# Graph network on one core: two of each tile's four adjacency scatters in the message pass, the others in edge order beside the first convolution

## The reference, cut to what matters

```python
x = _layernorm(x + _L0_gnn_ref(x, src, dst, ...))                 # softmax over the edges of a node
x = _layernorm(x + _L1_gnn_ref(x, edge_index, edge_attr_4, ...))  # a message of each edge, summed
x = _layernorm(x + _L2_gnn_ref(x, edge_index, ...))               # two convolutions, relu between
x = _layernorm(x + _L3_gnn_ref(x, edge_index, ...))               # two convolutions, elu between

def _sage_conv(h, src, dst, Wl, bl, Wr, num_nodes):
    agg = _mean_aggr(h, src, dst, num_nodes)   # mean of h[src] over the edges that end at a node
    return agg @ Wl.T + bl + h @ Wr.T
```

## Time and profile before

| | |
|---|---|
| median of 3 runs | 5566.3 us (5557.26 to 5571.82) |
| the profiled execution, its own time | 5569.94 us |
| its span, first to last instruction | 5568.1 us |
| mean granted TensorE clock | 0.818 |
| PE, DVE, ACT, POOL busy | 58%, 49%, 28%, 45% |

### The profile page before, as it was taken

How to read it: one execution, slowest core, us unless ns; L and a number is a source line. 1 busy time by engine, 2 the same in 40 slices (tenths; PEclk the granted TensorE clock), 3 DMA queues, 4 the chain that set the end, 5 groups by cost and what they waited for, 6 DMA issues and landing times.

```text
span 5568.1 us, 71606 instructions
## 1 busy us (share of the span) xinstructions
PE 3216.9 (58%) x18541; PEld 2357.2 (42%) x18541; DVE 2708.7 (49%) x6211; ACT 1578.4 (28%) x3821; POOL 2483.5 (45%) x2580
## 2 busy tenths in 40 slices
PE   0444444444464454454444445443118999999999
PEld 0333233333343333333333333332106887778877
DVE  3777777777644444444444444436313234433333
ACT  1666666666222222222222222222000001111000
POOL 6555555555555566656555655666760000000000
PEclk9999999999986666666666666655558999999999
DMA  6555555555223333333333333332014666666676
GB/s 202 168 178 181 166 180 180 170 178 168 64 73 87 87 97 89 87 87 90 86 91 84 95 88 89 85 88 54 2 44 172 248 249 247 245 249 251 254 276 231
DMA packets 411992, 801.65 MB, mean 144 GB/s; under 512 B 237480, under 2 KB 288396, under 8 KB 385692
## 3 DMA queue, kind: packets, MB, share of 16 engines
q1 hardware_dynamic: 263894, 591.99, 31.8%
q0 software_dynamic: 82320, 90.28, 7.8%
q10 hardware_dynamic: 65718, 118.62, 5.6%
HBM read 581.84 MB, written 218.74 MB: 144 GB/s over the span
## 4 chain that ended last, share of the span: by engine, by line
another core or an unknown queue 30%; PE 27%; issue 17%; ACT 12%; DVE 8%; ACTq 3%; POOL 1%; SPq 1%; DMA 0%; DVEq 0%; POOLq 0%
PE ps L991 22%; ACT ps L1040 2%; ACT dump L1044 2%; ACT out_ring L1056 2%; ACT relu_dump L1040 2%; DVE second L1474 2%; ACT second L1081 1%; PE ps L953 1%; ACT out_ring L1064 1%; ACTq L1066 1%; DVE area L1490 1%; ACT ps L1076 1%; ACTq L1060 1%; DVE second L1484 1%
## 5 line engine op out<-in xcount | busy, mean ns | idle before, releaser
L843 PE MATMUL ps<-ident,area 96*128 96x96 f32 x2352 | 441.3, 355 | 1154.6 <-ACT out_ring L1056 425.5
L693 POOL DMA_INDIRECT area<-src_table,idx_src x784 | 750.5, 957 | 525.1 <-DMA idx_src<-src_dram 270.3
L693 POOL DMA_INDIRECT area<-relu_table,idx_src x784 | 739.5, 943 | 537.3 <-issue 336.1
L843 PEld LDWEIGHTS ps<-ident,area 96*128 96x128 f32 x2352 | 352.1, 211 | 1281.3 <-issue 957.8
L1461 DVE TENSOR_TENSOR_SCAN area<-flags,area,ps 96x512 f32<-96x512 int8 x196 | 249.8, 1274 | 1213.5 <-ACT dump L1044 1007.4
L704 POOL DMA_INDIRECT adj<-copies_ring,cell_ring x587 | 578.1, 985 | 378.0 <-DVE cell_ring L1442 198.4
L991 PE MATMUL ps<-early,area 128*128 128x288 bf16 x5194 | 665.8, 287 | 1.6 <-DVE early L1606 1.6
L991 PE MATMUL ps<-second,area 128*128 128x288 bf16 x5194 | 651.2, 286 | 0.5 <-DVE second L1606 0.5
L991 PEld LDWEIGHTS ps<-early,area 128*128 128x128 f16 x5194 | 508.9, 98 | 129.8 <-issue 2.1
L991 PEld LDWEIGHTS ps<-second,area 128*128 128x128 f16 x5194 | 508.2, 98 | 128.1 <-DVE second L1606 1.1
L1426 DVE SCALAR_TENSOR_TENSOR second<-second,area,ps 128x512 bf16<-128x512 f32 x784 | 538.6, 743 | 0.0
(11 more groups left out here) (298 smaller groups left out, 4555.1 us busy)
## 6 DMA issues: line engine op xcount, KB each, us to landing
area<-adj SPq DMA_DIRECT2D x196, 1632.0 KB
adj<-early SPq DMA_DIRECT2D x102, 816.0 KB
soft_sums<-out_ring ACTq DMA_DIRECT2D x196, 384.0 KB
second<-key_dram SPq DMA_DIRECT2D x98, 512.0 KB
area<-dst_table SPq DMA_DIRECT2D x784, 48.0 KB
sums<-out_ring ACTq DMA_DIRECT2D x196, 192.0 KB
second<-caps_dram SPq DMA_DIRECT2D x98, 192.0 KB
attr<-attr_parts SPq DMA_DIRECT2D x196, 72.0 KB
```

The source lines that it names most:

```text
L693: pool.indirect_dma_start(out=src_rows[:, s, c, :], out_offset=None, in_=gather_table[p], in_offset=bass.IndirectOffsetOnAxis(ap=idx_src[s ...
L843: last = nc.tensor.transpose(ps[:, b, c * F:(c + 1) * F], r[:, (s * CH + c) * P:(s * CH + c + 1) * P], ident[0:F, 0:F])
```

## The change

`NOW` becomes 2, and in tile t the message pass scatters chunks 2t and 2t+1 of the sorted edges, whose copies were counted in a tile already done. So the 196 tiles scatter the first 392 chunks (`EARLY`), half of all. The other 390 are scattered by POOL after the gathers of the ends, in edge order, in batches of eight (`BATCH`), and after each batch has landed POOL raises `adj_ready`. DVE prepares them in one go after the pass (`cell_late`, `copies_late`, in the space of `out_ring`). A table `tile_ready` of 49 numbers, made from the degrees in the setup by three small DVE operations, tells how many batches each row of tiles needs.

The first convolution no longer waits for the joint rows. SP's `fill_first` loads 49 blocks of row j when the batches that it needs are there (a register loaded from `tile_ready`), PE's `sum_up_first` sums them, and DVE's `hold` adds the result, times `rdeg`, to `z_sb`. Then the two joint rows are summed, which needs all batches. Then comes a second step for all 49 tiles: SP loads the two columns of tying blocks of all rows in one DMA (`links`, pieces of 512 bytes), PE's `link` multiplies them with the parts of the joint rows (six matmuls a tile), DVE's `post` adds the result to `z_sb` into `layer_out`, and PE turns and projects it for the second convolution, with ACT and DVE as in the first projection. `over_jobs` takes its number of jobs as an argument, ACT evicts tile k before it keeps the z of tile k-1, and the search in the setup waits for its rows two groups at a time, which frees semaphores. The later convolutions are as before.

```diff
 REPEAT = 1024
-NOW = CH - 1
+NOW = 2
...
+    EARLY = ET * NOW
+    LATE = CN - EARLY
+    BATCHES = math.ceil((SCATTERS - EARLY) / BATCH)
+    assert LATE > 0 and SCATTERS > EARLY
...
+        def over_first_jobs(step, eng):
+            over_jobs(step, eng, jobs=NT, head=SLOTS + 1)
+
+        def uses_of_slot(lane, q):
+
+            return (len(range(lane, NT, SLOTS)) + (1 if lane < EXT else 0) + len(range(lane, JOBS, SLOTS)) * (q - 1)) if q else 0
...
 
 
-            sp.wait_ge(adj_made, 16 * (SCATTERS + EXT))
             sp.wait_ge(node[-1]["kept"], NG)
-            for q in range(CONVS):
+
+            def fill_first(j, lane, nth):
+                if not (isinstance(j, int) and j < SLOTS):
+                    sp.wait_ge(conv["summed_up"], j - (SLOTS - 1))
+                batches = nc.values_load(tile_ready[0:1, bass.ds(j, 1)], engines=[mybir.EngineType.SP], min_val=1,
+                                         max_val=BATCHES + 1)
+                sp.wait_ge(adj_ready, batches)
+                sp.dma_start(slots[:, lane, 0:NT, :].rearrange("p b n -> p (b n)"),
+                             adj[bass.ds(j, 1), :, 0:NT * P].rearrange("a p c -> (a p) c")).then_inc(slot_landed[lane], 16)
+
+            over_first_jobs(fill_first, sp)
+
+            sp.wait_ge(adj_ready, BATCHES + 1)
+            for i in range(EXT):
+                sp.wait_ge(conv["summed_up"], NT - SLOTS + 1 + (i - NT) % SLOTS)
+                sp.dma_start(slots[:, i, 0:NT, :].rearrange("p b n -> p (b n)"), adj[NT + i, :, 0:NT * P])\
+                  .then_inc(slot_landed[i], 16)
+            sp.wait_ge(conv["summed_up"], NT - 1)
+            sp.dma_start(links, adj[0:NT, :, NT * P:KB * P].rearrange("t p (e n) -> p t e n", e=EXT)).then_inc(links_landed, 16)
+
...
-                    pool.sem_inc(scatters_begun, 1)
+                    pool.sem_inc(dmas_begun, 1)
                     for c in range(NOW):
-                        if isinstance(u, int) and (u * RING + s) * CH + c >= SCATTERS:
-                            return
                         pool.indirect_dma_start(
                             out=adj_all, out_offset=bass.IndirectOffsetOnAxis(ap=cell_ring[:, s, c:c + 1], axis=0),
...
-                    pool.wait_ge(last_redirected, 2)
-                    for c in range(NOW, SCATTERS, CH):
-                        pool.indirect_dma_start(
-                            out=adj_all, out_offset=bass.IndirectOffsetOnAxis(ap=cell[:, c:c + 1], axis=0),
-                            in_=copies_last[:, c // CH:c // CH + 1], in_offset=None).then_inc(adj_made, 16)
+                    pool.wait_ge(late_redirected, 2)
+
+                    def batch_done(i):
+                        begun = sum(min(BATCH, SCATTERS - EARLY - k * BATCH) for k in range(i % 2, i + 1, 2))
+                        pool.wait_ge(late_made[i % 2], 16 * begun)
+                        pool.sem_inc(adj_ready, 1)
+
+                    pool.wait_ge(adj_made, 16 * (EARLY + EXT))
+                    pool.sem_inc(adj_ready, 1)
+                    for i in range(BATCHES):
+                        for c in range(i * BATCH, min((i + 1) * BATCH, SCATTERS - EARLY)):
+                            pool.indirect_dma_start(
+                                out=adj_all, out_offset=bass.IndirectOffsetOnAxis(ap=cell_late[:, c:c + 1], axis=0),
+                                in_=copies_late[:, c:c + 1], in_offset=None).then_inc(late_made[i % 2], 16)
+                        if i:
+                            batch_done(i - 1)
...
-            for q in range(CONVS):
+            y = parts_of_y[0]
+
+            def sum_up_first(j, lane, nth):
+                pe.wait_ge(slot_landed[lane], nth * 16 + 16)
+
+                wait(pe, conv["reduced"], j - 1)
+                if isinstance(j, int) and j == 0:
+                    pe.wait_ge(conv["split"], NT)
+                for s in range(NT):
+                    last = nc.tensor.matmul(bank(lane % 2, P, PARTS_F), slots[:, lane, s, :],
+                                            y[:, s, :, :].rearrange("p c f -> p (c f)"), start=s == 0, stop=s == NT - 1)
+                last.then_inc(conv["summed_up"], 1)
+
+            over_first_jobs(sum_up_first, pe)
+
+            for i in range(EXT):
+                pe.wait_ge(slot_landed[i], 16 * uses_of_slot(i, 1))
+                pe.wait_ge(conv["reduced"], NT + i - 1)
+                for s in range(NT):
+                    last = nc.tensor.matmul(bank((NT + i) % 2, P, PARTS_F), slots[:, i, s, :],
+                                            y[:, s, :, :].rearrange("p c f -> p (c f)"), start=s == 0, stop=s == NT - 1)
+                last.then_inc(conv["summed_up"], 1)
...
+            pe.wait_ge(conv["extended"], EXT)
+
+            def link(k):
+
+                wait(pe, conv["posted"], k - 1)
+                for e in range(EXT):
+                    for c in range(PARTS):
+                        last = nc.tensor.matmul(bank(6 + k % 2, P, F), links[:, k, e, :], y[:, NT + e, c, :],
+                                                start=e == 0 and c == 0, stop=e == EXT - 1 and c == PARTS - 1)
+                last.then_inc(linked, 1)
+
+            for k in range(NT + 2):
+                if k < NT:
+                    link(k)
+                if 1 <= k <= NT:
+                    pe.wait_ge(conv["posted"], k)
+                    turn_into(1, k - 1, (k - 1) % 2, layer_out[:, (k - 1) % 2, :])
+                if k >= 2:
+                    project_into(1, k - 2, k % 2)
+
+            for q in range(1, CONVS):
...
 
-            for k in range(NT):
-                evict_into(0, k, k % 2)
-                keep_z(0, k, k % 2)
-
-            for q in range(CONVS):
+            def evict_and_keep_all(q):
+                for k in range(NT):
+                    evict_into(q, k, k % 2)
+                    if k:
+                        keep_z(q, k - 1, (k - 1) % 2)
+                keep_z(q, NT - 1, (NT - 1) % 2)
+
+            evict_and_keep_all(0)
...
+                    for s in range(RING):
+                        dve.wait_ge(sums_stored[s], 16 * EI * (p + 1))
+                    chain.do(v.tensor_scalar(is_late_repeat, copies[:, EARLY:CN], float(REPEAT), None, ALU.is_ge))
+                    chain.do(v.tensor_scalar(cell_late, cell[:, EARLY:CN], 0, None, ALU.bitwise_or))
+                    v.tensor_scalar(copies_late, copies[:, EARLY:CN], float(REPEAT), None, ALU.min)\
+                     .then_inc(late_redirected, 1)
+                    v.copy_predicated(cell_late, is_late_repeat, elsewhere_late).then_inc(late_redirected, 1)
 
...
-            for q in range(CONVS):
+            def reduce_job(j, lane, b):
+                dve.wait_ge(conv["summed_up"], j + 1)
+                v.tensor_reduce(whole[:, b, :], bank(lane % 2, P, PARTS_F).rearrange("p (c f) -> p f c", f=F), axis=X,
+                                op=ALU.add).then_inc(conv["reduced"], 1)
+                dve.wait_ge(conv["reduced"], j + 1)
+
+            z_of = lambda k: z_sb[:, bass.ds(k, 1), :].rearrange("p a f -> p (a f)")
+
+            def hold(j, lane, nth):
+                b = lane % 2
+                reduce_job(j, lane, b)
+                v.scalar_tensor_tensor(z_of(j), whole[:, b, :], rdeg[:, bass.ds(j, 1)], z_of(j), ALU.mult, ALU.add)\
+                 .then_inc(held, 1)
+
+            dve.wait_ge(conv["zkept"], NT)
+            over_first_jobs(hold, dve)
+            for i in range(EXT):
+                reduce_job(NT + i, NT + i, (NT + i) % 2)
+                split(whole[:, (NT + i) % 2, :], parts_of_y[0][:, NT + i, :, :], conv["extended"], i + 1)
+            dve.wait_ge(held, NT)
+
+            def post(k):
+                dve.wait_ge(linked, k + 1)
+
+                wait(dve, conv["turned"], two_back(NT, k))
+                v.scalar_tensor_tensor(layer_out[:, k % 2, :], bank(6 + k % 2, P, F), rdeg[:, k:k + 1], z_of(k), ALU.mult,
+                                       ALU.add).then_inc(conv["posted"], 1)
+
+            post(0)
+            for k in range(NT):
+                if k + 1 < NT:
+                    post(k + 1)
+                split_into(1, k, k % 2)
+
+            for q in range(1, CONVS):
 
...
```

73 lines of the change are left out of this document (46 added, 27 removed).

## The result

The changed kernel takes 5661.2 us (median of 4 runs) against 5569.1 for the kernel before in the same session: 1.0176 times, 95% interval 1.015 to 1.0202. It was forecast at 5459, with a range to 5640: 200 us off, and on the other side. The profiled execution has a span of 5659.3 us against 5568.1, 91 us more.

A forecast was written before the change was run, and what follows sets the result against it. The prediction took POOL's burst of DMA issues, with a tail of late signals behind it, to set the message pass's period. 5569.9 - 216 (pass) + 109 (later start of the second convolution) = 5463, taken as 5459 us; range 5340 to 5640.

The forecast's parts named there:

- The pass: Message pass: two scatters fewer in a pair of tiles save 2.2 us, over 98 pairs 216 us.
- a seventh for SP's queue: Message pass: the full 2.57 us a pair was cut by a seventh to 2.2, the index wait being SP's.
- rival 1: Full 252 us gain in the pass and good overlap after it: 5369 us; chance 0.20.
- Rival 2: SP's queue of thirteen DMAs bounds the message pass, gain only 0 to 60 us: 5615 to 5675 us; chance 0.13.
- Scatters: After the pass: 390 late scatters at 1.28 to 1.29 us, 503 us, the last issued at M + 579.
- M: Time at which the message pass ends, when the joint scatter is done; 3829.7 us in the profile before the change.
- Rival 4: Late scatters slow down to 1.506 us each beside DVE work, the last issued at M + 663: 5481 us; chance 0.05.
- Splits: Beside late scatters: two tiles may share one late signal, 4.15 us a tile; first convolution's jobs start at M + 310.
- Jobs: First convolution: 7.3 us a job beside scatters, 38 by M + 585, then 11 at 6.45, ending M + 656.
- Second step: After the jobs: joint rows 14 us, 49 tiles at 3.25 us, first fills 3; second convolution at M + 836, +109 us.
- Rival 3: Late signals hold the first convolution: 5588 us, or 5699 if none of it runs before the last scatter; chance 0.14.

The follow-up runs named there:

- Dve_extra: Changed kernel with six small DVE memsets ahead of the split of each tile: 5704.8 us, beside 5568.9 for the kernel before.
- now3: Changed kernel with three scatters of a tile in the message pass instead of two, leaving 194 late ones: ratio 1.0204 to the kernel before.
- no_late: Changed kernel without the 390 late scatters, POOL only raising the counts: 5163.2 us, ratio 0.935 to the kernel before.
- gathers: Changed kernel with each late scatter replaced by an indirect gather of 128 rows into SBUF: 5623.3 us, beside 5522.2 for the kernel before.
- memsets: Changed kernel with two POOL memsets in place of each late scatter: 5231.5 us, beside 5568.9 for the kernel before.
- after: The profiled execution of the changed kernel itself: span 5659.3 us, against 5568.1 for the kernel before.
- sync_batch: Changed kernel, but POOL waits for each batch of eight late scatters just issued to land, not the one before: ratio 0.9827 to the kernel before.
- pause_memset: Changed kernel with five chained POOL memsets after each batch of eight late scatters: 5487.9 us, beside 5459.2 for a repeat of sync_batch on the same chip.
- sync16: As sync_batch, with batches of 16 scatters, so 25 pauses instead of 49: ratio 1.0159 to the kernel before.

## Why the prediction was wrong, point by point

**The pass.** 216 us were forecast, 251 measured (245 on the second kind of chip). The deduction of a seventh for SP's queue was not needed: the tail moved with POOL's burst. Right in mechanism, mis-sized by 35 us; rival 1 had 252. Rival 2 falls.

**Scatters.** M + 579 forecast, M + 597 measured, since each took 1.33 us, not 1.285. Rival 4 doesn't show: a scatter took 0.984 us beside the splits (267.70/272 in the windows above), not 1.206, and the longer ones, 1.066 (126.81/119), lie beside the first jobs, where DVE has four instructions. The Trainium skill (SBUF — State Buffer, "Who interferes with whom") says that a VectorE instruction with two inputs in SBUF contends with a GpSimd instruction that reads SBUF. One of the five steps of a split is of that kind. On the second kind of chip, where all 49 splits lie in the first 88 us of the stream, a scatter takes 1.011 us there (the first three 1.46 to 1.66) and 0.970 beside the jobs: if this is that rule, it is worth 0.04 us a scatter at most.

**Splits.** This step failed first. I said that signals were late, and that two tiles could share one late signal: jobs from M + 310. They started at M + 432, since it stayed at 8.40 us a tile. Dve_extra shows what was wrong: the instructions of an engine come 0.70 to 1.40 us apart, so a step that takes none out brings nothing, and the removed wait of ACT did nothing there. (Without the stream that same order halves a split, 2.95 to 1.5 us.)

**Jobs.** This is the step that cost the sign. "Beside scatters the fill's issue or PE's signal may be late by up to 5.3 us, but four slots and two banks cover most of it; I take 7.3." Latency can be covered by buffers; a rate can't. A job is 98 instructions of PE, 98 x 1.40 = 137 us, 134 measured for the second. 38 jobs were to be done when the scatters end; it was 1.9, 91 matmuls. The first convolution ended at M + 907, not 656, 251 us later: 217 are the 36.1 jobs more that were left over, at 6.0 each, less 5 since the other 11 took 6.0 too and not 6.45; 12 are the longer stream (M + 597 for 585), and the other 27 the time until PE was back at its full pace. The second step gave 17 back. How much of it is the late start? With jobs from M + 432, but at 7.3 as forecast, 22.6 are done by M + 597 and the rest by M + 755, which with 163 for the second step is M + 918, 191 later than before: by this estimate the change would still have gained 60 us. The pace of the jobs made the loss. Could it have been told before? In the earlier trace rows the late engine stands idle, which fits both readings, but the trace of before has no long run of PE's instructions without a wait beside late scatters. The nearest thing was that the split's pace was exactly 8.40 us, tile after tile, which a late signal doesn't explain. 8.40 us over the six PE instructions of a tile is 1.40 each, and 98 x 1.40 = 137 us should have stood as the upper bound of a job beside scatters; no rival had a job slowed itself.

**Second step.** 180 us forecast with joint rows and the first fills, 162.6 measured; in now3, where the convolution overlaps nothing, the new way costs 118 us in all.

**Rival 3** came nearest, in its second version (no jobs before the last scatter, 5699); with the measured 251 for the pass it gives 5664, and 5661 were measured. That is in part luck: its jobs end at M + 896 and its second step takes 180, measured are 907 and 163, and late signals were not the cause. Its chance, 0.14 for both versions, was too low, on the strength of an order of ACT that concerned waits. On the second kind of chip the sum of the forecast nearly holds: 245 gained in the pass and 93 paid after it, where I had 216 and 109. The overlap that it counted on is there, but not its terms: splits take 1.5 us and not 4.15, jobs 6.0 and not 7.3, and after the first 24 jobs they follow the edge order.

**What is shown and what isn't.** Shown: it is the stream of indirect DMAs from POOL (no_late, gathers), not POOL being busy (memsets); what is slowed is PE's and DVE's own instructions (after, dve_extra); 2 us without an issue after eight DMAs lift nearly all of it (sync_batch, pause_memset), after sixteen about half (sync16); and on a second kind of chip it is missing. That the tails in the message pass are the same thing is likely from rows 4 to 6 and their absence on the second kind, but no run took them away on the first. What in the chip does it, whether it is POOL's making of the DMAs or their many small pieces, and whether plain DMAs do it too, stays open. It isn't the loading of code by DMA, a piece for each instruction: the page of the changed kernel counts 68 packets in all on its two instruction queues. The same section of the Trainium skill says that PE and ACT never wait on anyone, so by its rule the sharing of a port isn't the cause; PE, with 2.40 us of idle time before each matmul, is the engine that is slowed most here.

## What to carry to other kernels

Before work is put beside a stream of another engine, find in the trace a stretch in which an engine has many instructions and no waits beside that stream, and count its instructions a microsecond; an idle time that ends "remote" or "issue" fits a late signal and a slow supply alike, and only the second can't be buffered. An exact, constant pace of a loop under such a stream points to the supply. Where a stream of indirect DMAs must run beside a busy engine, short pauses in it can pay (49 of 2 us brought the second convolution forward by 201 us), if the burst between them is short enough; and a ratio of 1.02 on one chip may be 0.97 on the next, so the kernel before is timed beside on each.

## What the runs showed of the hardware

- On the first kind of chip, beside an unbroken stream of indirect DMAs from POOL, every 1.3 us, PE gets a matmul with its weight load each 2.80 us (0.12 without the stream), and DVE in dve_extra an instruction each 0.70 to 1.40 us; the first 34 matmuls after a long wait still run at full pace (after, gathers). It sets in some 25 us (41 before the change) after the start of the stream, and lasts 24 us beyond its end.
- Eight such DMAs and a pause of 1.97 us: hardly any slowing (7 us a job for 6.0; 2315 matmuls in 514 us, from about the 20th job with the edge order as the bound). Sixteen and the same pause: 312 in 382 us.
- Chips of two kinds: the kernel before takes 5520 to 5570 us on one, 4781 to 4785 on the other, with the same 0.958 and 0.986 us for POOL's issues, and the same 0.286 us for a matmul.
- 390 plain DMAs of 256 bytes from POOL's queue, 128 pieces of two bytes each, beside the 1.6 MB loads of another queue: these took 37.8 us to land.
